# A graph-network kernel on one core: the opening layer norm in seven slices, the histogram finished inside the first pass, and two pieces of the second pass moved ahead of its scatter

## The chip, the cores and the metric

The kernel runs on one core of one Trainium2 chip. The metric is device microseconds (us) of one execution. Engines are named as in the profile: PE is the matrix engine, DVE the vector engine, ACT the scalar engine, POOL the GpSimd engine and SP the sync engine, which here only issues transfers. Every engine runs its own list of instructions in order and waits on semaphores for the others.

## What is computed

The graph has 12,500 nodes with 64 features and 212,500 directed edges, sorted by destination (`dst`). Edge attributes (32 numbers) and edge weights come with each edge. Four graph layers work on the layer-normed node features and are added up. What matters here:

```python
m = mean(x); h = relu((x - m) / sqrt(var(x) + 1e-5))        # opening layer norm, per node
# layer 0: max over the edges of a node, in both directions
edge = h[src] * (1 + coef * w)                               # and the same with src and dst exchanged
pooled = relu(edge @ pool_w.T + pool_b); pooled[src == dst] = -inf
agg = maximum(segment_max(pooled, other_end), 0)
x = x + relu(concat([h, agg]) @ final_w.T + final_b)
# layers 1 to 3 (not touched here): four dense graph convolutions, a message sum, an edge MLP
...
```

The kernel multiplies the node table by `pool_w` before the gather (the scale of an edge can be applied afterwards), and needs the edges once in order of `dst` and once in order of `src`; it sorts them itself by counting.

## The kernel before

The 12,500 nodes are padded to 98 blocks of 128 rows (`NJ = 98`), the edges to 1664 tiles of 128. An edge chunk is 8 tiles, so there are 208 chunks (`NCH = 208`, `NIT = 52` rounds of four). One indirect transfer of POOL moves one tile: 128 rows, with one row number per partition.

**Front.** SP queues all inputs, the whole `x` first (L499). DVE builds constants (L1961 to L1977), waits for every parameter, and then runs `norm(1)` (L1986) over all 98 blocks at once: sum, scale, subtract, square, sum, scale, reciprocal, multiply, with one square root on ACT. PE, ACT and DVE then project the normed rows by `poolw` in seven slices of 14 blocks (`project_pairs`, `pairs_in`, `pairs_out`), DVE copies each slice to `T` (L2041), and SP writes it to the table in HBM (L538). After that SP loads the first row numbers (L596), and DVE zeroes `Z` and splits the node numbers into digits of 7 bits (L2042 to L2054).

**Pass one** (`step1` on each engine, `gather_pass` on POOL and SP). For each chunk POOL gathers 8 tiles of the table (L833). DVE scales and masks them (`pre1`, L2085 and L2087), PE turns them (L969), ACT applies the relu (L1583), DVE takes a running maximum along runs of equal `dst` (`scan1`, L2070), PE turns them back (L978), ACT copies (L1510) and SP writes the rows (L557). In the same steps DVE builds one-hot rows of the digits for two half chunks (`onehots`, L2063), and PE adds them up as a histogram in two PSUM banks (`hist`, L1078). POOL may run up to four chunks ahead of `pre1` (`g_used`). ACT also queues, at every second chunk, zeros for the table `fill_rows` and for the adjacency matrix `adj` (`zeroes`, L1575 and L1570).

**Between the passes.** When the last chunk is done, PE closes the histogram (L1096), DVE turns counts into starts (L2115 to L2133, with PE at L1101 and L1106), and from these into row numbers (L2143 to L2155) and degrees (L2157 to L2162). POOL then scatters the 98 blocks of `T` to the first edge row of each node (`fill64`, L848). SP waits for that, copies one more row (L628), and starts the loads of pass two.

**Pass two** (`step2`). For each chunk SP loads rows of `fill_rows` (L637), masks (L551) and edge attributes (L646); DVE scans them (`scan2`), PE turns them (L1178), ACT scales them into records (`messages`, L1631) together with weights and digits (`payload`, L1612 to L1614). In parallel the *position chain* of a chunk finds where each record goes in the order by `src`: one-hot rows (L2173), PE products with the running counts (L1130 to L1156), ACT copies (L1620, L1626), DVE look-ups (L2190) and the integer row numbers (`pos`, L2200). POOL scatters the eight tiles of the chunk to `records` (L863). ACT's list has `payload` of a later chunk ahead of the second half of a chunk's messages, and `payload` waits for the scatter of the chunk that used the same of four buffers. After the first four chunks ACT writes the inverse degrees to HBM, 4 bytes at a time (L1668).

**After pass two** POOL gathers the ends of 98 blocks of runs of pass one into `T` (`ends`, L881), scatters 480 tiles of matrix cells to `adj` (L908), gathers the 98 blocks of run ends of pass three (L881), and scatters the other 1184 tiles. SP and DVE meanwhile read the records back, make the cells (`cells_made`, L2276 to L2331) and run pass three (`step3`). The dense layers read `adj`; their first group waits for the last cells (SP at L749, POOL's count at L900).

The order that matters most is POOL's own list:

```python
gather_pass("g_used", 0, 0, 16, TP)
pool.wait_ge(sem("fill_zero"), 16 * NCH // 2)
pool.wait_ge(*dve_at("rows_ready"))
# 98 indirect scatters to fill64, then 208 x scatter(it, i)
runs_done(1)
# wait for all records
ends(T, runs_l064, endrow[0], 0)
```

## Time and profile before

| | |
|---|---|
| three timed runs | 9992.73, 10000.24, 10000.26 us (median 10000.24) |
| the profiled execution, its own time | 9970.27 us |
| its span in the profile | 9968.5 us, so 1.8 us lie around it |
| first gather of pass one | 96.08 us |
| last gather of pass one, first fill scatter | 2226.94 us, 2254.86 us |
| last fill scatter, first record scatter | 2379.77 us, 2403.97 us |
| last record scatter, first run-end gather | 4539.48 us, 4542.60 us |
| last matrix cell | 6963.1 us |

A row of the timeline gives start, duration, engine, line, operation, tiles and count, and in brackets the idle time of the engine before it and what ended that. Times are counted from the start of the span.

### The profile page before, as it was taken

The numbers are of one execution on the slowest core, as the hardware profiler recorded it, in microseconds if no ns is written. First come the engines' busy times: TensorE is split into PE (matmuls) and PEld (weight loads), VectorE is DVE, ScalarE is ACT, GpSimd is POOL, SyncE is SP. The second block draws the span as 40 slices with busy tenths as digits, with TensorE's granted clock in tenths as the row PEclk, the third lists the DMA queues.
The fourth block names the chain that finished last, engine by engine and source line by source line (L and its number), as shares of the span: only waits on it lengthen the run. The fifth ranks groups of instructions, "written<-read, shape, count | busy, mean of one in ns | idle before, by whom it ended". The sixth has DMA issues, their size and how long they took to land.

```text
span 9968.5 us, 151706 instructions
## 1 busy us (share of the span) xinstructions
PE 7021.8 (70%) x44134; PEld 5746.9 (58%) x44134; DVE 7055.7 (71%) x18556; ACT 4861.0 (49%) x7947; POOL 5378.0 (54%) x5426
## 2 busy tenths in 40 slices
PE   3444444442888788782656567994899999997998
PEld 2333333332666667661445455662699898896787
DVE  6777777773766666663558777773788787787777
ACT  1111111111555555551542336883688787785777
POOL 4777777776777777777777777777000000000220
PEclk6555555556777766775876888997999999999999
DMA  4555555553333333339995896773788888886999
GB/s 147 167 170 173 167 170 167 169 165 49 93 92 94 93 92 93 92 94 80 274 235 122 196 214 176 203 204 86 200 281 280 249 281 256 273 282 179 209 216 198
DMA packets 2775231, 1739.56 MB, mean 175 GB/s; under 512 B 1805014, under 2 KB 2613948, under 8 KB 2774372
## 3 DMA queue, kind: packets, MB, share of 16 engines
q1 hardware_dynamic: 2435172, 1298.36, 51.7%
q10 hardware_dynamic: 165920, 277.72, 7.8%
q0 software_dynamic: 173408, 154.46, 6.6%
q8 instruction: 370, 6.06, 0.3%
q14 instruction: 361, 2.96, 0.1%
HBM read 1065.70 MB, written 506.69 MB: 158 GB/s over the span
## 4 chain that ended last, share of the span: by engine, by line
POOL 43%; PE 24%; issue 19%; DMA 7%; DVE 4%; ACT 2%; SPq 1%; POOLq 0%; DVEq 0%; ACTq 0%
PE PS L1307 16%; POOL adj L908 16%; POOL records L863 13%; POOL G L833 12%; PE PS L1497 3%; DMA pair_raw<-adj 2%; PE PS L1287 1%; DMA G<-node_table,IDX 1%; DMA raw_f<-adj 1%; ACT ring_f L1918 1%; DMA records<-RT,IDX 1%; POOL AG L881 1%; POOL T L881 1%; DMA IDX<-in_src_q 1%; DVE OH L2063 1%
## 5 line engine op out<-in xcount | busy, mean ns | idle before, releaser
L833 POOL DMA_INDIRECT G<-node_table,IDX x1664 | 1625.0, 977 | 601.5 <-issue 591.5
L908 POOL DMA_INDIRECT adj<-OH,EA x1664 | 1649.0, 991 | 507.4 <-issue 507.4
L863 POOL DMA_INDIRECT records<-RT,IDX x1664 | 1614.7, 970 | 545.0 <-issue 498.0
L1307 PE MATMUL PS<-ring_f,terms_r 128*128 128x448 f32 x8232 | 1701.1, 368 | 17.1 <-DVE ring_f L2569 10.8
L2569 DVE CAST ring_f<-raw_f 128x1792 fp32r<-128x1792 uint8 x1323 | 1404.9, 1091 | 376.0 <-DMA raw_f<-adj 186.3
L1795 ACT CAST ring_f<-raw_f 128x1792 fp32r<-128x1792 uint8 x882 | 1468.8, 1692 | 372.1 <-DMA raw_f<-adj 217.9
L1307 PEld LDWEIGHTS PS<-ring_f,terms_r 128*128 128x128 f32 x8232 | 1541.2, 188 | 166.1 <-DVE ring_f L2569 21.0
L1156 PE MATMUL PS<-R 98*128 98x128 f32 x3328 | 989.8, 390 | 0.0
L2070 DVE TENSOR_TENSOR_SCAN S<-M,S,PS 128x512 f32<-128x512 bf16 x621 | 790.9, 1274 | 229.3 <-ACT PS L1684 207.4
L1078 PE MATMUL PS<-OH 128*98 128x128 bf16 x3328 | 453.5, 317 | 630.2 <-DVE OH L2063 630.2
L927 POOL DMA_INDIRECT HC<-node_table,srow x21 | 30.5, 1450 | 1537.2 <-issue 1537.2
L2457 DVE SCALAR_TENSOR_TENSOR AG<-AG,PS 128x1792 bf16<-128x1792 uint8 x294 | 592.5, 2021 | 342.7 <-DMA AG<-adj 202.4
L2063 DVE TENSOR_SCALAR OH<-iota_b,AG 128x128 bf16<-128x128 bf16 (+1 forms) x4480 | 833.5, 284 | 0.0
L1078 PEld LDWEIGHTS PS<-OH 128*98 128x98 bf16 x3328 | 365.7, 198 | 796.7 <-DVE OH L2063 796.7
L2181 DVE TENSOR_TENSOR L<-PS,below 128x512 bf16<-128x512 f32 x416 | 285.4, 686 | 730.4 <-PE PS L1140 726.3
L1583 ACT ACTIVATE PS<-PS,poolb 128x512 f32<-128x512 f32 x208 | 137.7, 662 | 1252.7 <-PE PS L969 1189.4
L945 POOL DMA_INDIRECT ends_b<-runs_e,endrow_src x98 | 149.0, 1520 | 1049.8 <-PE PS L1319 547.9
L1156 PEld LDWEIGHTS PS<-R 98*128 98x128 f32 x3328 | 711.0, 264 | 0.0
L1154 PE MATMUL PS<-OH 128*98 128x128 bf16 x1664 | 473.0, 284 | 313.4 <-ACT R L1626 311.5
L1497 PE MATMUL PS<-ring_f,terms_r 128*128 128x448 f32 x2744 | 611.2, 377 | 68.8 <-DVE ring_f L2783 31.4
L1918 ACT CAST ring_f<-pair_raw 128x1792 fp32r<-128x1792 uint8 x343 | 571.6, 1693 | 170.1 <-PE PS L1497 109.8
L969 PE MATMUL PS<-ident,RT 128*128 128x128 f32 x832 | 231.8, 434 | 597.9 <-DVE RT L2087 596.9
(406 smaller groups left out, 14435.3 us busy)
## 6 DMA issues: line engine op xcount, KB each, us to landing
raw_f<-adj SPq DMA_DIRECT2D x2205, 224.0 KB, 3.6
adj<-Z ACTq DMA_DIRECT2D x105, 1568.0 KB
AG<-adj SPq DMA_DIRECT2D x735, 224.0 KB
G<-records SPq DMA_DIRECT2D x624, 128.0 KB
M<-same_dst SPq DMA_DIRECT2D x416, 128.0 KB
fill_rows<-Z ACTq DMA_DIRECT2D x104, 512.0 KB, 2.9
runs_l<-R SPq DMA_DIRECT2D x208, 256.0 KB
G<-fill_rows SPq DMA_DIRECT2D x208, 256.0 KB
```

Of the source, the lines that this page charges most:

```text
L833: pool.indirect_dma_start(G[:, i, q * D:(q + 1) * D], None, table, bass.IndirectOffsetOnAxis(ap=IDX[:, i, q:q + 1], axis=0)).then_inc(sem( ...
L863: pool.indirect_dma_start(rec, bass.IndirectOffsetOnAxis(ap=IDX[:, i, q:q + 1], axis=0), RT[:, i, q, :], None).then_inc(sem(f"scattered{i} ...
L908: pool.indirect_dma_start(adj_cells, bass.IndirectOffsetOnAxis(ap=CELL[:, at:at + 1], axis=0), VAL[:, at:at + 1], None).then_inc(sem(f"cel ...
L1078: t = pe.matmul(hist_of(b, k % 2 if b == 0 else 0), OH[:, s, 2 * b, k, 0:NJ], OH[:, s, 2 * b + 1, k, :], start=False, stop=False, skip_gro ...
L1156: t = pe.matmul(bank(6 + x)[:, k * P:(k + 1) * P], OHTs[0:NJ, x, k * P:(k + 1) * P], Cs[0:NJ, k, :], start=False, stop=True, skip_group_ch ...
L1307: m = pe.matmul(half_of(x, h)[:, c, :], stat, RINGF[q % NR][:, h * QW + c * HW:h * QW + (c + 1) * HW], start=K == 0, stop=False, skip_grou ...
L1497: m = pe.matmul(half_of(0, h)[:, c, :], stat, RINGF[n % NE][:, h * QW + c * HW:h * QW + (c + 1) * HW], start=p == 0, stop=p == AB - 1, ski ...
L1795: act.copy(RINGF[q % NR][:, :], RAWF[q % NW][:, :]).then_inc(sem("conv_a"), 1)
L1918: act.copy(RINGF[n % NE][:, :], raw[:, 0:2 * QW, K % 2]).then_inc(sem("conv_a"), 1)
L2063: t = dve.tensor_scalar(OH[:, s, d, k, 0:w], iota_b[:, 0:w], key(d, q + k), None, ALU.is_equal)
L2070: return dve.tensor_tensor_scan(S[:, i % 2, :], mask, data, init, op0, op1)
L2569: dve.tensor_copy(RINGF[q % NR][:, :], RAWF[q % NW][:, :]).then_inc(sem("conv_d"), 1)
```

## The change

1. **Front.** `x` is loaded in four parts, the first ahead of everything, with `poolw` after the second. The opening norm runs in seven slices of 14 blocks: DVE `centred` and `spread`, the square on ACT instead of DVE (`squared`), the root per slice, DVE `normed`; PE turns and projects a slice as soon as it is normed, and ACT instead of DVE copies the product to `T` (`pair_copied`). The first four loads of row numbers go ahead of the table writes. `DX`, the input of the same-run masks, lies in `Z` instead of `G`.
2. **Histogram.** Chunk `c` of pass one takes half chunks `HLO[c]` to `HLO[c+1]`, 9 for every 4 chunks, so all are done at chunk `CH = 185`; the counts become starts, row numbers and degrees in steps of chunks 185 to 192 (one call for each chunk). ACT's zeros of `fill_rows` go out in the first 104 chunks, those of `adj` at every second chunk as before.
3. **Extra row.** SP's copy of one row to `fill_rows` (with its two waits) moves from behind the fill scatter into round 39 of pass one; POOL's fill scatter waits for it.
4. **Position chains.** The chains of chunks 0 to 3, with their payloads and one-hot rows, come first in the lists of PE, DVE and ACT; the scans and messages of these chunks follow.
5. **Run ends.** POOL gathers the first 14 of the 98 run-end blocks between the fill scatter and the records, after a wait for the fill's landing; 84 stay behind the records.
6. Two helpers for ordering (`Steps`) are replaced by the common one (`then`), with the same waits.

```diff
-            load(X[:, :], a["x"])
+            x_in(0)
+            x_in(1)
+            sp.wait_ge(*dve_at("w_zero"))
+            for h in range(2):
+                sp.dma_start(poolw[h * D:(h + 1) * D, h * D:(h + 1) * D], a["poolw_t"]).then_inc(sem("x_in1"), 16)
+            x_in(2)
...
+            for i in range(4):
+                chunk_idx(i, i)
+            table_parts(UA)
             sp.wait_ge(*dve_at("md_ready"))
...
+                    if it == NIT * 3 // 4:
+                        sp.dma_start(dh[0:1, 0:1], a["dst_ext"][:, H + 1:H + 2]).then_inc(sem("dh_then_v"), 16)
...
+                        sp.dma_start(fill64[1:2, :], table[bass.ds(node_h, 1), :]).then_inc(sem("fill_b"), 16)
...
             pool.wait_ge(sem("fill_zero"), 16 * NCH // 2)
+            pool.wait_ge(sem("fill_b"), 16)
             pool.wait_ge(*dve_at("rows_ready"))
...
+            runs_done(1)
+            pool.wait_ge(sem("filled"), 16 * NJ)
+            ends(T, runs_l064, endrow[0], 0, 0, 2)
...
-            ends(T, runs_l064, endrow[0], 0)
+            ends(T, runs_l064, endrow[0], 0, 2, NG)
...
+            for s in range(NG2 + 3):
+                if s < NG2:
+                    squared(s)
+                if 1 <= s <= NG2:
+                    first_root(s - 1)
+                if 2 <= s <= NG2 + 1:
+                    pair_in(s - 2)
+                if s >= 3:
+                    pair_copied(s - 3)
...
+            for s in range(NG2 + 2):
+                if s < NG2:
+                    centred(s)
+                if 1 <= s <= NG2:
+                    spread(s - 1)
+                if s >= 2:
+                    normed(s - 2)
...
+            def step1(c):
+                pre1(c // 4, c % 4)
+                for h in range(HLO[c], min(HLO[c] + 1, HLO[c + 1])):
+                    onehots(h * KC, h % 2, h, 4)
+                if c:
+                    scan1((c - 1) // 4, (c - 1) % 4, c == 1)
+                for h in range(HLO[c] + 1, HLO[c + 1]):
+                    onehots(h * KC, h % 2, h, 4)
+                if c == CH + 1:
+                    starts_by_row()
...
+                payload(0, i, True)
+                for x in range(2):
+                    half(i, i, x, None, None, False)
+            for i in range(4):
+                act.wait_ge(sem("back2"), i + 1)
+                for q0 in range(0, 8 if i < 3 else 4, 2):
+                    messages(i, i, q0)
+            payload(1, 0, False)
             act.wait_ge(sem("oh_ready"), 2 * NCH + 1)
             act.dma_start(dinv_n.rearrange("o (j p) -> (o p) j", p=P), dinv[:, :], allow_slow_non_contiguous=True).then_inc(sem("dinv_out"), 16)
```

## Rows read from the trace of the kernel before

**Rows 1.** The page: POOL in 40 slices, and the chain that ended last.
```profile
POOL 4777777776777777777777777777000000000220
...
POOL 43%; PE 24%; issue 19%; DMA 7%; DVE 4%; ACT 2%; SPq 1%; POOLq 0%; DVEq 0%; ACTq 0%
```
**Rows 2.** The waits of POOL: us in total, times, longest us.
```profile
POOL fill_rows L848 <- DVEq L2156: 27.0, 1, 27.0
POOL records L863 <- ACT RT L1614: 23.2, 1, 23.2
POOL records L863 <- ACT RT L1631: 23.1, 27, 10.9
```
**Rows 3.** The lines of POOL's gathers and scatters: duration min/median/max, first and last start.
```profile
L833 POOL DMA_INDIRECT G<-node_table,IDX x1664: 940/944/2557, 96.1 to 2226.9; - x185
...
L863 POOL DMA_INDIRECT records<-RT,IDX x1664: 965/969/1048, 2404.0 to 4539.5; - x185
```
**Rows 4.** The timeline of the front, 0 to 135 us.
```profile
32.75 0.15 DVE L1981 TENSOR_SCALAR w12r<-w12c 64x1 f32<-64x1 f32 x1 [28.09 <-DMA wls<-in_ws]
...
35.15 6.68 DVE L1988 TENSOR_REDUCE nd<-X 128x98 f32<-128x6272 f32 x1
...
35.97 1.28 ACT L1554 ACT_TABLE_LOAD   x1
...
70.55 3.22 PE L1044 MATMUL PS<-ident,Hn 128*128 128x128 f32 x14 [35.21 <-DVEq L1998]
...
89.61 1.09 DVE L2041 TENSOR_SCALAR T<-PS 128x896 f32<-128x896 f32 x1 [0.47 <-PE PS L1037]
```
**Rows 5.** Busy time by stretch, 5 to 10 us: PE, PEld, DVE, ACT, POOL, clock, DMA, GB/s.
```profile
5.00:10.00 5.00, 0.00 (x0) 0.00 (x0) 0.00 (x0) 0.00 (x0) 0.00 (x0) 1.00 0.95 408
```
**Rows 6.** The timeline of DVE late in the kernel, a norm of one 14-block slice.
```profile
9105.35 1.09 DVE L2668 TENSOR_REDUCE nd<-X 128x14 f32<-128x896 f32 x1
9106.47 0.17 DVE L2669 TENSOR_SCALAR nd<-nd 128x14 f32<-128x14 f32 x1
...
9110.51 0.24 DVE L2675 RECIPROCAL nd<-na 128x14 f32<-128x14 f32 x1 [0.28 <-ACT na L1872]
```
**Rows 7.** Groups of ACT's instructions by shape: busy us, mean ns of one, idle before.
```profile
L1744 ACT ACTIVATE R<-Hn,pcols 128x896 f32<-128x896 f32 x20 | 22.7, 1134 | 29.8 <-DVEq L2432 28.4 <-DVEq L2532 1.4
...
L1533 ACT ACTIVATE G<-PS,pcols 128x896 f32<-128x896 f32 x7 | 7.7, 1097 | 17.1 <-PE PS L1044 17.1
```
**Rows 8.** The timeline of DVE near the end of pass one: two chunk starts.
```profile
2222.59 0.69 DVE L2085 TENSOR_TENSOR RT<-G,EA 128x512 f32<-128x512 f32 x1 [4.64 <-DMA G<-node_table,IDX]
...
2230.44 0.69 DVE L2085 TENSOR_TENSOR RT<-G,EA 128x512 f32<-128x512 f32 x1 [0.16 <-DMA G<-node_table,IDX]
```
**Rows 9.** The page's group of the one-hot rows of pass one (416 half chunks).
```profile
L2063 DVE TENSOR_SCALAR OH<-iota_b,AG 128x128 bf16<-128x128 bf16 (+1 forms) x4480 | 833.5, 284 | 0.0
```
**Rows 10.** The timeline behind the fill scatter: its last instruction, SP's first load.
```profile
2379.77 0.98 POOL L848 DMA_INDIRECT fill_rows<-T,begrow  x1 [0.30 <-issue]
...
2384.05 0.37 SPq L637 DMA_DIRECT2D G<-fill_rows  x1
```
**Rows 11.** DMA issues of 2380 to 2480 us: KB, us to landing.
```profile
dinv_n<-dinv ACTq DMA_DIRECT2D x1, 49.0 KB, 40.2
```
**Rows 12.** The timeline around the run ends: POOL's first gather, DVE's cells, POOL's first cell.
```profile
4542.60 0.98 POOL L881 DMA_INDIRECT T<-runs_l,endrow_dst  x1 [2.16 <-DMA records<-RT,IDX]
...
4643.38 0.56 DVE L2322 CAST OH<-EA 128x768 uint8<-128x768 int32 x1
...
4672.37 1.00 POOL L908 DMA_INDIRECT adj<-OH,EA  x1 [0.30 <-issue]
```
**Rows 13.** The timeline later: DVE's last step before POOL's second run ends, and these.
```profile
5231.06 0.17 DVE L2362 CAST dcol<-vcol 128x7 int32<-128x7 f32 x1
...
5291.72 0.99 POOL L881 DMA_INDIRECT AG<-runs,endrow_src  x1 [0.30 <-issue]
```
**Rows 14.** The waits of SP, 6000 to 7000 us.
```profile
SPq L749 <- POOLq L900: 126.3, 3, 79.0
```

More of the change, by code:

```diff
@@ L1080, in hist @@
                 t.then_inc(sem("hist_done"), 1)
-            def step1(it, i, first):
-                c = it * 4 + i
-                fwd(i, Gs[:, i % 2, :], c, sem("gs_ready"), c + 1)
-                hist(c * 2, 0)
-                if not (first and i == 0):
-                    back((i - 1) % 4, c - 1, c - 1)
-                hist(c * 2 + 1, 1)
-            for i in range(4):
-                step1(0, i, True)
-            for it in range(1, NIT):
-                for i in range(4):
-                    step1(it, i, False)
@@ L1109, in count_of @@
+            for c in range(NCH):
+                step1(c)
+            back(3, NCH - 1, NCH - 1)
             def count_of(h):
@@ L1189, in _ @@
             pe.wait_ge(*dve_at("starts_in"))
-            fwd2(0, 0)
             turn(0, 0)
@@ L1193, in _ @@
             for i in range(4):
-                step2(0, i, False)
+                for x in range(2):
+                    chain(i, i, x, False)
+            fwd2(0, 0)
+            for i in range(4):
+                back2(i, i)
+                fwd2((i + 1) // 4, (i + 1) % 4)
             for it in range(1, NIT - 1):
@@ new lines, in starts_in_all @@
+            def starts_in_all():
+                dve.wait_ge(*pe_at("row_offs"))
+                then(dve.tensor_copy(hoff[0:NJ, :], bank(5)[0:NJ, P:P + 2]))
+                for i in range(2):
+                    then(dve.tensor_tensor(HC[0:NJ, 2 + i, :], HC[0:NJ, 2 + i, :], HC[0:NJ, i, :], ALU.subtract))
+                    dve.tensor_scalar(HC[0:NJ, 2 + i, :], HC[0:NJ, 2 + i, :], hoff[0:NJ, i:i + 1], None, ALU.add)\
+                       .then_inc(sem("starts_ready"), 1)
+                dve.wait_ge(sem("starts_ready"), 2)
+                dve.tensor_tensor(HC[0:NJ, 4, :], HC[0:NJ, 4, :], HC[0:NJ, 3, :], ALU.add).then_inc(sem("starts_ready"), 1)
@@ L2136, in row_of, with starts_by_node @@
+            def starts_by_node():
+                dve.wait_ge(*pe_at("starts_t"))
+                for i in range(2):
+                    dve.tensor_copy(cnt[i][:, :], starts_of(i))
+                    then(dve.tensor_copy(beg[i][:, :], starts_of(2 + i)))
+                dve.sem_inc(sem("dve_at"), 1)
             def row_of(dst, e, w):
@@ new lines, in degrees, with step1 @@
+            def degrees():
+                dve.wait_ge(sem("root_out"), NG2 + 1)
+                then(dve.reciprocal(dinv[:, :], na[:, :]))
+            def step1(c):
+                pre1(c // 4, c % 4)
+                for h in range(HLO[c], min(HLO[c] + 1, HLO[c + 1])):
+                    onehots(h * KC, h % 2, h, 4)
+                if c:
+                    scan1((c - 1) // 4, (c - 1) % 4, c == 1)
+                for h in range(HLO[c] + 1, HLO[c + 1]):
+                    onehots(h * KC, h % 2, h, 4)
+                if c == CH + 1:
+                    starts_by_row()
+                if c == CH + 2:
+                    starts_in_all()
+                if c == CH + 3:
+                    starts_by_node()
+                if c == CH + 4:
+                    rows_of_nodes(0)
+                if c == CH + 5:
+                    rows_of_nodes(1)
+                if c == CH + 6:
+                    first_rows()
+                if c == CH + 7:
+                    degrees()
@@ L2165, in onehots2 @@
+            for c in range(NCH):
+                step1(c)
+            scan1(NIT - 1, 3, False)
             def onehots2(h, s):
@@ L2211, in scan2, with step2 @@
                 dve.sem_inc(sem("pt_free"), 1)
-            def step2(it, i, first, last):
+            def step2(it, i, last):
                 c = it * 4 + i
@@ L2216, in step2 @@
                 end = last and i == 3
-                scan2(it, i, first and i == 0)
-                if not (first and i == 0):
+                scan2(it, i, False)
+                if c != 4:
                     look(h - 1, c - 1, (i - 1) % 4, 1)
```

302 lines of the change are left out of this document (155 added, 147 removed).

## The prediction

> **What bounds the kernel now.** I read the page's slices and its chain first, then POOL's waits, then the timelines around each of those waits. In the slices POOL stands at seven tenths from 96 us to about 6960, and the chain gives POOL 43% and "issue" 19% [rows 1]. Seven tenths is POOL at its limit: one indirect transfer takes 0.944 (gather) or 0.969 us (scatter), and 0.30 us of issue follow each of them [durations in rows 3, the issue in rows 10], so a tile costs 1.247 to 1.27 us, and POOL has 1664 + 98 + 1664 + 98 + 1664 + 98 of them in a line. So up to 6963 us the time is set by POOL's list, and only holes in that list can be closed. POOL's waits show them: 27.0 us ahead of the fill scatter, 23.2 us ahead of the records, 23.1 us over 27 waits among the records, with one of 10.9 [rows 2]; besides, everything ahead of the first gather at 96.1 us [rows 3].
>
> **Front.** Now DVE idles 28.09 us until all parameters are there, then runs five operations of 6.68 us over all 98 blocks, one after the other, and only then PE and ACT begin [rows 4]. The change cuts this into seven slices. `x` is no limit: the loads run at 408 GB/s [rows 5], so the first slice (448 KB) is there at about 3 us and all of `x` (3136 KB) at about 10, while DVE's constants take it to 4.7. A slice costs DVE what a later norm of the same shape shows: 1.12 us for each big operation from start to start, 0.20 for a small one, 0.27 for the reciprocal [rows 6]. Without the square, that is four big, two small and a reciprocal, 4 x 1.12 + 2 x 0.20 + 0.27 = 5.1 us, and 36 us for seven. ACT has per slice a square (1.13, by its nearest row with a source in SBUF), a root (0.2), the relu (1.10) and the copy (0.9 to 1.1) [rows 7], together 3.5 us, so DVE sets the pace; a few waits where ACT's ordered list meets DVE's add about 2 us. DVE ends at 4.7 + 36 + 2 = 42.5. The last slice still goes through PE (1.6 us for seven products at the slow rate of 3.22 per 14 [rows 4]), the relu, PE again (1.4) and the copy, with hops 5 to 6 us: 48. Today the last copy ends at 90.7 [rows 4] and POOL starts 5.4 us behind it; the row numbers are loaded earlier now, but the table write has to land as before, so I keep 5 and put the first gather at 52.5. **Gain 43.5 us**, bounds 38 (waits in every slice) and 47 (none, and PE at its fast rate).
>
> ACT has run no Square in this trace. The trace shows one table load of 1.28 us when ACT first takes a root, and none when relus and copies follow [rows 4]. If Square and Sqrt lay in different sets, each slice would pay two loads, 2.56 us more on ACT, which then sets the pace; worked through the slices this ends 4 us later. The Trainium skill, "ScalarE: Activation LUTs", section "Table sets: the hidden batching unit", asks to group calls by set, which the slices would break; by its price of about 2.7 us a switch the front would end some 22 us later, an estimate. I take no load; the case is rival F.
>
> **Pass one.** The histogram's half chunks rise from 2 to 9/4 per chunk until chunk 185. DVE needs 7.85 us for a chunk when it doesn't wait (from 2222.59 to 2230.44 [rows 8]), and a half chunk of one-hot rows is 833.5 / 416 = 2.0 us of DVE [rows 9], 2.6 with its gaps. On average that makes 7.85 + 0.25 x 2.6 = 8.5 us, in a chunk with three halves 10.5, against POOL's 2131.8 / 208 = 10.25. POOL may be four chunks ahead, so one long chunk in four is covered, and the pass keeps POOL's pace. The number of one-hot rows is the same in all, so what they do to POOL (a mean of 977 ns against a median of 944) stays. The starts, row numbers and degrees move beside the gathers: some 45 small DVE instructions, about 13 us, which fill half of the 27.0 us gap now [rows 2]. They ran while POOL waited, so their effect on a gather is not in the trace; the nearest is the second half of the run ends, where 98 gathers take 129.8 us for 98 x 1.247 = 122.2 while DVE makes cells for 40 us [rows 12], 7.6 us lost. By that share I put 1.5 us on the starts and the position chains together; bounds 0 and, were POOL blocked for as long as DVE works, 13. SP's two waits for the extra row hold its list for some 5 us once; the row numbers are loaded three chunks (30 us) ahead, so nothing. Fill zeros in the first 104 chunks only move traffic, and DMA is not what POOL waits for; nothing.
>
> **Between the passes.** When the last gather ends, the row numbers are there since chunk 192, and the 27.0 us [rows 2] shrink to an issue gap: **gain 26.5 us**, unless DVE lags by 15 chunks.
>
> **Behind the fill scatter.** Its 98 tiles stay (126 us); the chains of four chunks lie beside them. At pass two's rate, 2135 us for 208 chunks [rows 3], four take 41 us, with pass one's last chunk ahead of them some 60, so they end long before. Today SP's first load goes 3.3 us after the last fill tile (the extra row is in it) and the first record 19.9 us after that load [rows 10, 3]. Now POOL waits some 1.5 us for the landing, then has 14 gathers of 1.247, 17.5 us, and could take records 19.3 us after the last fill tile. The messages must be ready by then: load, scan, turns and eight ACT operations. That took at most 1.8 + 19.9 = 21.7 us when the chain ran in between, and without the chain I estimate 12 to 13. So 19.3 against 23.2: **gain 3.9**, bounds 1.5 and 4.2. **The 14 gathers leave their old place: gain 17.5.** There POOL gets to the first cell scatter 17.5 us earlier against the records; today DVE has the cells ready at 4644 and POOL comes at 4672 [rows 12], so 28 us of cover less 17.5, still 10 in hand. At the second run ends DVE was done at 5231 and POOL came at 5292 [rows 13], 60 us in hand. At the end SP waits 126 us for cells [rows 14], so the dense layers take the whole shift.
>
> **The hole among the records.** The 10.9 us come at chunk 4, where ACT's `payload` waits for the scatter of chunk 1, which lands late because the inverse degrees, in pieces of 4 bytes, take 40.2 us to land [rows 11]. That transfer is still issued after four chunks, now as soon as chunk 0 has landed, some 4 us earlier against the records. I take a gain of 2, bounds 0 and 15.
>
> **Sum:** 43.5 + 26.5 + 3.9 + 17.5 + 2 - 1.5 = 91.9, so 92 us. Against the profiled execution's own 9970.27 that is 9878; the median of the runs is 30 us above it, and I set the gain against the median: 10000.24 - 92 = **9908 us**. What a measurement here can tell from no change is 0.2%, 20 us.
>
> **Rivals.**
> *A, a new wait takes the 17.5.* The cells come later than I think, because the read-back of the records now shares DMA with POOL's cell scatter. For it: only 10 us are in hand. Against it: the read of the first cells ends before POOL gets there. 10000.24 - 92 + 17.5 = 9926.
> *B, the hole closes.* If the late landing no longer meets ACT, all 15 us of it go: 10000.24 - 92 - 13 = 9895.
> *C, DVE blocks POOL.* If a transfer could not be issued while DVE works, 13 us of starts and four chains of about 7 us (some seven tenths of a chunk) would be paid in full, 41 us: 9948. Against it stands the record scatter: with a busy DVE its median is 969 ns and its longest of 1664 is 1048 [rows 3]; for it, a gather of 2557 ns [rows 3]. The Trainium skill, "SBUF — State Buffer", section "Who interferes with whom", speaks for it: a vector operation in a two-port mode, or with two inputs in SBUF, keeps GpSimd out for the whole instruction. By that rule it is the moved small operations, not the one-hot rows, that would cost.
> *D, the early histogram misses.* DVE lags so far that row numbers come at the old place: 26.5 back, 9935. DVE's 8.5 us against 10.25 speaks against it.
> *E, slower: DVE becomes pass one's bound.* If a chunk cost DVE over 10.25 us on average, POOL would wait for `g_used` in 185 chunks. It turns the change into a loss above 10.25 + 92 / 185 = 10.75; at 11 us the pass grows by 139 and the time is 10047. It needs 2.5 us a chunk that the timeline doesn't show.
> *F, ACT changes tables in every slice.* The 4 us above: 9912. Against it: relu and copy forced no load behind the root [rows 4]; Square itself is not shown.
>
> **How the numbers follow.** Forecast 0.64, F 0.06, A 0.10, B 0.09, C 0.05, D 0.04, E 0.02. The forecast's own terms spread from 38 to 47 in the front, from 0 to 13 in what DVE costs POOL; with A and B that makes 9885 to 9930. I widen it to 9880 to 9932, since the profiled execution lies 30 us under the median. All cases but E are faster by over 20 us: faster 0.96; E and some mixture of C, D and A leave 0.02 for no change and 0.02 for slower.
>
> **What would show it.** First gather near 52 us; the fill scatter right behind the last gather, with no wait; the first record about 19 us behind the last fill tile, with 14 gathers in between; 84 gathers behind the records and no wait ahead of the first cell; a mean of L833 that stays under 0.985 us. Wrong would be a POOL waiting for `g_used` in pass one (E), a mean of over 1 us (C), or a wait ahead of the cells (A).

## The result, and the profile after

The changed kernel takes 9901.15 us (median of 4 runs, 9889.59 to 9904.07), the kernel before 9998.43 us in the same rounds (4 runs, 9992.73 to 10000.26): a ratio of 0.9906, 95% interval 0.9894 to 0.9919, so 97 us less. The forecast was 9908, 92 us less than the 10000.24 known then. The profiled execution of the changed kernel took 9903.3 us, with a span of 9901.5.

Both kernels were profiled a second time later. From the starts of POOL's transfers every term of the forecast can be read as a difference; all times in us, the first and the second profile of each kernel side by side:

| term, start to start | before | changed | forecast | measured |
|---|---|---|---|---|
| first gather | 96.1, 96.2 | 55.0, 54.1 | 43.5 | 41.0, 42.1 |
| pass one, first to last gather | 2130.9, 2130.5 | 2139.4, 2134.5 | -1.5 | -8.5, -4.1 |
| last gather to first fill tile | 27.9, 28.0 | 1.2, 1.2 | 26.5 | 26.7, 26.7 |
| the 98 fill tiles | 124.9, 124.9 | 125.2, 125.2 | 0 | -0.3, -0.3 |
| last fill tile to first record | 24.2, 24.5 | 20.5, 20.5 | 3.9 | 3.7, 4.0 |
| first to last record | 2135.5, 2138.4 | 2133.4, 2130.9 | 2 | 2.1, 7.5 |
| last record to first adj cell | 132.9, 131.8 | 114.9, 114.6 | 17.5 | 18.0, 17.2 |
| first to last cell | 2290.7, 2290.2 | 2288.8, 2290.1 | 0 | 1.9, 0.1 |
| **up to the last cell** | 6963.1, 6964.4 | 6878.4, 6871.2 | **91.9** | **84.7, 93.2** |
| last cell to the end | 3005.4, 3020.0 | 3023.1, 3018.8 | 0 | -17.7, 1.2 |

The page of the changed kernel: the 40 slices of POOL, the chain that ended last, and the groups that answer to [rows 1, 3].

```profile
POOL 5777777777777777777777777776000000001220
...
POOL 43%; PE 19%; issue 18%; DMA 10%; DVE 5%; ACT 4%; SPq 1%; POOLq 0%; ACTq 0%; DVEq 0%
...
L853 POOL DMA_INDIRECT G<-node_table,IDX x1664 | 1633.5, 982 | 560.5 <-issue 548.7
...
L907 POOL DMA_INDIRECT records<-RT,IDX x1664 | 1614.9, 970 | 519.8 <-issue 497.7
```

POOL is still the bound up to the last cell: the same seven tenths and the same 43% of the chain. What is left of idle time shows in POOL's waits (us in all, times, the longest), which answer to [rows 2]:

```profile
POOL G L853 <- issue: 548.7, 1625, 53.7
...
POOL records L907 <- ACT RT L1677: 21.7, 30, 8.7
...
POOL T L884 <- DMA fill_rows<-T,begrow: 2.0, 1, 2.0
```

The wait of 27.0 us ahead of the fill scatter and that of 23.2 us ahead of the records are gone, the first gather waits 53.7 us instead of 95, and among the records there is still one of 8.7. The joints in POOL's timeline (start, duration; in brackets the idle time before it and its releaser):

```profile
2194.39 0.94 POOL L853 DMA_INDIRECT G<-node_table,IDX  x1 [0.30 <-issue]
2195.64 1.02 POOL L869 DMA_INDIRECT fill_rows<-T,begrow  x1 [0.30 <-issue]
...
2320.83 0.98 POOL L869 DMA_INDIRECT fill_rows<-T,begrow  x1 [0.30 <-issue]
2323.79 0.99 POOL L884 DMA_INDIRECT T<-runs_l,endrow_dst  x1 [1.98 <-DMA fill_rows<-T,begrow]
...
2340.10 0.94 POOL L884 DMA_INDIRECT T<-runs_l,endrow_dst  x1 [0.30 <-issue]
2341.35 1.00 POOL L907 DMA_INDIRECT records<-RT,IDX  x1 [0.30 <-issue]
...
4588.39 0.94 POOL L884 DMA_INDIRECT T<-runs_l,endrow_dst  x1 [0.30 <-issue]
4589.64 1.00 POOL L931 DMA_INDIRECT adj<-OH,EA  x1 [0.30 <-issue]
```

Every joint but the landing of the fill tiles is a bare issue of 0.30 us: the row numbers are there when the last gather ends, the messages when the 14 run ends are through, the cells when the other 84 are. So the parts of the change do what they say. Three rows of the table are off: the front gave 1.4 to 2.5 us less than forecast, pass one is 4 to 9 us longer, and in the first pair of profiles 18 us are missing behind the last cell, where the change does nothing. And one row, then as now, deserved more attention than it got: a mean gather of 0.982 us (0.977 before) against a median of 0.944 [rows 3] is 1664 x 0.038 = 63 us of pass one.

**Where those 63 us sit.** DVE and POOL around one long gather of the changed kernel, from the timelines of the two engines:

```profile
1004.54 0.69 DVE L2158 TENSOR_TENSOR RT<-G,EA 128x512 f32<-128x512 f32 x1 [4.29 <-DMA G<-node_table,IDX]
1005.26 0.69 DVE L2160 TENSOR_TENSOR RT<-RT,EA 128x512 f32<-128x512 f32 x1
1005.87 1.35 DVE L2136 TENSOR_SCALAR OH<-iota_b,AG 128x98 bf16<-128x98 bf16 x8
...
1004.25 0.94 POOL L853 DMA_INDIRECT G<-node_table,IDX  x1 [0.30 <-issue]
1005.49 1.28 POOL L853 DMA_INDIRECT G<-node_table,IDX  x1 [0.30 <-DMA IDX<-in_src_q]
1007.08 1.00 POOL L853 DMA_INDIRECT G<-node_table,IDX  x1 [0.30 <-issue]
```

The gather at 1004.25 was under way before the multiply began and took 0.94 us. The one at 1005.49 started inside the add, which had 0.46 us to run, and took 0.34 longer. Counted over all 1664 gathers: in 220 of them one of the two operations was running, or began, within 0.05 us of the gather's start, and these lose 57.1 us; the other 1444 lose 5.5. In the kernel before it is 46.8 us in 214, and 7.4 in the rest. The loss follows the time that the operation has left at the gather's start: 0.2 to 0.3 us left cost 0.12 on average, 0.4 to 0.5 cost 0.32, 0.6 to 0.7 cost 0.50; an operation that begins later in the gather costs 0.03 us at most. That this is a cause and not a coincidence, the first two experiments show.

### The profile page after: what moved, and what is told of

Read it like the earlier page. It is cut to its first block, busy times and chain, and to the rows that moved or that the text cites. A ratio compares the mean times of both kernels' runs of the same rounds, so it can differ in the third digit from the quotient of the medians.

```text
span 9901.5 us, 151767 instructions
## 1 busy us (share of the span) xinstructions
PE 7084.5 (72%) x44134; PEld 5794.4 (59%) x44134; DVE 7040.9 (71%) x18590; ACT 4876.1 (49%) x7967; POOL 5382.8 (54%) x5426
## 4 chain that ended last, share of the span: by engine, by line
POOL 43%; PE 19%; issue 18%; DMA 10%; DVE 5%; ACT 4%; SPq 1%; POOLq 0%; ACTq 0%; DVEq 0%
POOL adj L931 16%; POOL records L907 12%; PE PS L1342 12%; POOL G L853 12%; DMA raw_f<-adj 3%; DMA pair_raw<-adj 3%; PE PS L1532 2%; ACT ring_f L1848 2%; DMA G<-node_table,IDX 1%; DVE OH L2136 1%; PE PS L1322 1%; POOL fill_rows L869 1%; POOL T L884 1%; POOL AG L884 1%; DMA records<-RT,IDX 1%
## 5 line engine op out<-in xcount | busy, mean ns | idle before, releaser
L1342 PEld LDWEIGHTS PS<-ring_f,terms_r 128*128 128x128 f32 x8232 | 1534.4, 188 | 180.2 <-ACT ring_f L1848 24.5
L1187 PE MATMUL PS<-R 98*128 98x128 f32 x3328 | 1010.0, 397 | 0.0
```

The lines of the kernel that those rows point to most:

```text
L1187: t = pe.matmul(bank(6 + x)[:, k * P:(k + 1) * P], OHTs[0:NJ, x, k * P:(k + 1) * P], Cs[0:NJ, k, :], start=False, stop=True, skip_group_ch ...
L1342: m = pe.matmul(half_of(x, h)[:, c, :], stat, RINGF[q % NR][:, h * QW + c * HW:h * QW + (c + 1) * HW], start=K == 0, stop=False, skip_grou ...
```

## Experiments

Each kernel is the changed one with the edit named, unless it says otherwise. Spans and stretches are those of the kernel's own profile; beside them stand the times of the changed kernel's two profiles.

**1. Multiply and add of pass one on ACT.**

```diff
-                pre1(c // 4, c % 4)
...
+                scaled(c)
                 relu1(c % 4, c)
...
+                for q in range(8):
+                    t = act.activation(Gs[:, i % 2, q * D:(q + 1) * D], G[:, i, q * D:(q + 1) * D], ACT.Identity,
+                                       scale=s_q[:, c * 8 + q:c * 8 + q + 1], bias=pen_q[:, c * 8 + q:c * 8 + q + 1])
```

> The two DVE operations per chunk that multiply and add with both sources in SBUF (128x512 each, 0.69 us) become eight operations of 64 columns on ACT. Theory 1 (a DVE operation with two sources in SBUF holds up a gather that wants SBUF at its start or some 0.7 us into it; in the changed kernel 126 of 129 gathers of over 1.1 us overlap the add): the long gathers go, the mean of the 1664 gathers falls from 0.982 to about 0.95 us, pass one from 2139 to about 2090, the time to about 9852. Theory 2 (long gathers come from the DMA queues, the add only happens to follow a landing): mean and pass one stay within 5 us, the time at 9901. Where ACT became late, POOL would wait for the scaled chunks and the pass would be longer than 2139.

**2. The same on DVE with one source in SBUF.**

```diff
-                dve.tensor_tensor(o, g, bc(s_q[:, bass.ds(q, 8)], [P, 8, D]), ALU.mult)
-                dve.tensor_tensor(o, o, bc(pen_q[:, bass.ds(q, 8)], [P, 8, D]), ALU.add)
+                for k in range(8):
+                    t = dve.tensor_scalar(Gs[:, i % 2, k * D:(k + 1) * D], G[:, i, k * D:(k + 1) * D],
+                                          s_q[:, q + k:q + k + 1], pen_q[:, q + k:q + k + 1], ALU.mult, ALU.add)
```

> The multiply and the add of pass one become eight DVE operations of 64 columns with one source in SBUF and two scalars per partition. Theory 1 (only operations with two sources in SBUF hold a gather up): as with the work on ACT, a mean gather of about 0.95 us, pass one about 2090, the time about 9852. Theory 1b (any DVE operation does while it runs): the long gathers go, since each operation is some 0.1 us, but many gathers are longer by up to 0.1, a mean of about 0.96, pass one about 2105. Theory 2 (the DMA queues): no change, 2139 and 9901.

The group of the gathers on the page, with the work on ACT, then with one source on DVE:

```profile
L853 POOL DMA_INDIRECT G<-node_table,IDX x1664 | 1577.6, 948 | 561.1 <-issue 546.7
```

```profile
L853 POOL DMA_INDIRECT G<-node_table,IDX x1664 | 1579.6, 949 | 564.1 <-issue 540.8
```

The mean falls from 982 to 948 and 949 ns, and the gathers of over 1.1 us from 129 to 3 and 4. Pass one takes 2083.5 and 2092.3 us (of the latter some 5.5 us are waits of POOL for a chunk's row numbers), the time 9841.35 and 9847.5. So theory 1 holds: the two operations with both sources in SBUF cost pass one some 50 us. For the kernel before, where no run takes them away, the count above says 46.8. Theory 1b asked for a mean of 0.96 us and is out at that size: over the usual 0.944, all gathers together lose 8.8 us here and 6.8 with the work on ACT. That leaves some 2 us for the 1664 short operations, so a few nanoseconds for a gather are not excluded. The expectation named a second moment, 0.7 us into a gather; for these two operations the count above shows only the start, and what looked like the second was the multiply just ahead of the add. Longer operations with one source do have a second moment (experiment 7).

**3. The late histogram, twice.** Two half chunks per chunk, starts and row numbers behind pass one:

```diff
-        HLO = [min(2 * NCH, c * 9 // 4) for c in range(NCH + 1)]
-        CH = HLO.index(2 * NCH)
+        HLO = [2 * c for c in range(NCH + 1)]
+        CH = NCH - 1
...
             scan1(NIT - 1, 3, False)
+            starts_by_row()
...
+            degrees()
```

> The changed kernel with two half chunks of the histogram per chunk again and the starts, row numbers and degrees behind the last chunk of pass one; the front, the fill zeros, the chains and the 14 run ends stay as changed. Both theories: the gap between the last gather and the first fill tile comes back, from 1.2 to about 27 us. They differ on pass one, which took 2139.4 us in the changed kernel against 2130.9 before. Theory 1 (the extra DVE work of the early histogram moves DVE's operations against POOL's gathers, and more of them collide): the pass goes back to about 2131, the time rises by about 18 us to 9919. Theory 2 (the fill zeros, all in the first 104 chunks now, slow the gathers): it stays at about 2139, and the time rises by 27 us to 9928.

> The kernel with the late histogram once more. Its first pass one took 2137.3, but in that execution the median record scatter was 0.972 instead of 0.969, so all POOL work 0.3% longer, which is 5 us of that. Theory 1 (the early histogram shifts DVE's two-source operations against the gathers): with a record median of 0.969 pass one takes 2130 to 2133, as in the kernel before (2130.9 and 2130.5). Theory 2 (the fill zeros in the first half, or another part that stays changed here): 2135 to 2139, as in five profiles with the early histogram.

The gap comes back in full, in POOL's waits of the first run:

```profile
POOL fill_rows L868 <- DVEq L2222: 28.2, 1, 28.2
```

28.2 us where before has 27.0 [rows 2], so the histogram's term is confirmed. The times were 9940.43 and 9931.06, above what either theory said (9919 and 9928). Pass one took 2137.3 and 2132.4; all POOL work was some 0.3% longer in both executions (the median record 972 ns against 969 and 970), so the median of 0.969 that the second expectation asked for did not come. Leaving that out, the gathers that take over 0.02 us more than the usual 0.944 lose 57 and 52 us here, 56 to 62 in five profiles with the early histogram, and 54 and 53 in the two of the kernel before. That points to theory 1, at some 5 us, but the spread within one kernel is as large. What differs is a class of gathers that meet a whole operation (0.56 to 0.61 us longer, the multiply beginning at most 0.05 us behind their start): 26 and 25 in the two profiles of the changed kernel, none before, 10 and 4 here. Why the three-half chunks put the multiply there is not settled. Theory 2 has nothing for it: in the changed kernel's first profile the chunks 8 to 103, beside which the fill zeros run, lose 26.8 us, the chunks 104 to 199 lose 29.7.

**4. Both kernels once more**, with no edit.

> The kernel before, unchanged, profiled once more. In its first profiled execution the stretch behind the last adj cell took 3004 us and the whole 9970, 30 us under the median of its runs; the changed kernel's stretch took 3022, though the change does nothing there. Theory 1 (that first execution was a short one): behind the last cell now 3015 to 3030, up to the last cell 6964 within 5 us. Theory 2 (the change costs the dense layers 18 us): 3004 again, and the 30 us missing up to the last cell. The sum of the terms up to the last cell is the same by both, 84.7 us.

> The changed kernel, unchanged, profiled once more, for the spread of three terms. First gather: 55.0 in the first profile, 51.8 in two kernels with the same front, 55.6 in a third; if the last table write meets ACT's first adj zeros by chance, either value may come. Pass one: 2139.4; theory 1 (collisions of DVE's two-source operations with gathers come by phase) lets it fall anywhere from 2131 to 2141, theory 2 (the early histogram or the fill zeros cost 8 us) gives 2139 within 1.5. Behind the last cell: 3015 to 3030.

Behind the last cell, start of that cell to the end, the kernel before took 3020.0 us this time, the changed one 3018.8. So the 18 us missing there in the first pair are the short execution of the kernel before, and no cost of the change. Up to the last cell the two profiles of before agree within 1.3 us. The first gather of the changed kernel came at 54.1, pass one took 2134.5.

**5. No run ends ahead of the records.**

```diff
-            runs_done(1)
-            pool.wait_ge(sem("filled"), 16 * NJ)
-            ends(T, runs_l064, endrow[0], 0, 0, 2)
...
-            ends(T, runs_l064, endrow[0], 0, 2, NG)
+            runs_done(1)
+            ends(T, runs_l064, endrow[0], 0, 0, NG)
```

> The changed kernel with none of the 14 run-end gathers ahead of the records: all 98 come behind them again. Theory 1: POOL idles behind the last fill tile until the messages of chunk 0 are written, some 11.5 us (they were there at 2333.3, the last fill tile ended at 2321.8), so the first record comes 7.8 us earlier against the fill than with 14 gathers between, and the first cell 17.5 us later against the last record; together 9.7 us slower, about 9911. Rival (the two gains of the forecast are separate, 3.9 and 17.5): 21.4 slower, about 9922. What the 14 gathers are worth is the idle time that they fill, not their own length.

9910.99 us. POOL's waits behind the fill:

```profile
POOL records L904 <- ACT RT L1675: 20.5, 3, 11.6
```

POOL idles 11.6 us until the first messages are there, and the last record to the first cell takes 133.2 us again. From the last fill tile to the first record 12.6 us against 20.5, from the last record to the first cell 133.2 against 114.6: 18.6 - 7.9 = 10.7 us lost, near the 9.7 of theory 1. The 17.5 us that the forecast booked as one gain and the 3.9 that it booked as another are one thing: the 14 gathers fill 11.6 us of idle time, of which 2.0 go for the landing that they wait for.

**6. The inverse degrees written out beside the fill scatter.**

```diff
+            act.wait_ge(sem("oh_ready"), 2 * NCH + 1)
+            act.dma_start(dinv_n.rearrange("o (j p) -> (o p) j", p=P), dinv[:, :], allow_slow_non_contiguous=True).then_inc(sem("dinv_out"), 16)
             oht_copy(0, 0)
             for i in range(4):
                 payload(0, i, True)
...
             payload(1, 0, False)
-            act.wait_ge(sem("oh_ready"), 2 * NCH + 1)
-            act.dma_start(dinv_n.rearrange("o (j p) -> (o p) j", p=P), dinv[:, :], allow_slow_non_contiguous=True).then_inc(sem("dinv_out"), 16)
```

> The changed kernel with the write of the inverse degrees (pieces of 4 bytes, 40 us to land) issued beside the fill scatter instead of behind the messages of chunk 3. Theory 1 (the two holes among the records, 4.5 and 8.7 us, come because that write delays the landing of the records that ACT's payload waits for): both go, first to last record takes 2120 instead of 2133.4, the fill scatter stays at 125.2, and the time falls by 13 us. Rival (the write delays the fill tiles in the same way): the wait behind the last fill tile, 1.98 us, or the fill itself grows by as much. Rival 2 (the holes come from four chunks of messages being late by themselves): they stay.

POOL's waits from the fill to the last record:

```profile
POOL records L907 <- ACT RT L1677: 10.4, 34, 0.3
...
POOL T L884 <- DMA fill_rows<-T,begrow: 2.0, 1, 2.0
```

No wait among the records is longer than an issue any more, first to last record takes 2121.5 instead of 2133.4 and 2130.9, and neither the wait for the fill tiles nor the fill (125.5 against 125.2) has grown. So the holes were the landing of the 4-byte pieces [rows 11], as the forecast read them, and they cost 9 to 12 us. The time, 9898.41, shows less of it: the stretch behind the last cell, where the edit does nothing, took 3028.1 us against 3023.1 and 3018.8, and the cells before it 2292.0 against 2288.8 and 2290.1.

**7. The last layer's weights behind the table writes.**

```diff
-            load(l3w1[:, :], a["l3w1"])
-            load(l3w2[:, :], a["l3w2"])
...
             table_parts(UA)
+            load(l3w1[:, :], a["l3w1"])
+            load(l3w2[:, :], a["l3w2"])
```

> The two loads of the last layer's weights, whose issue takes SP 8 us, go behind the seven table writes in SP's list; DVE's digits and ACT's first adj zeros, which wait for the parameters, come some 10 us later with them. Theory 1 (the first gather comes at 55.0 instead of the 52.5 forecast because the table writes start at 33.5 where the first slice is ready at 26, and the last one shares DMA with the adj zeros): the writes start at about 26, the last lands 4 us after its issue at 45, the first gather at about 50, the time 4 to 5 us lower, 9897. Rival (a table write takes 10 us to land whatever is beside it): first gather at 55. What could go wrong: the digits end at about 71 instead of 59, and POOL, which can be four chunks ahead, would wait for the first scaled chunk if that came after about 91.

9894.93 us. The writes start at 28.3, the first gather comes at 51.7, but the first gathers are long. POOL, then DVE:

```profile
55.65 1.90 POOL L853 DMA_INDIRECT G<-node_table,IDX  x1 [0.30 <-issue]
57.85 3.30 POOL L853 DMA_INDIRECT G<-node_table,IDX  x1 [0.30 <-issue]
61.45 1.82 POOL L853 DMA_INDIRECT G<-node_table,IDX  x1 [0.31 <-issue]
...
57.54 1.55 DVE L2115 MEMSET Z<- 128x1792 f32 x1 [0.44 <-DVE vpos L2081]
59.01 0.96 DVE L2119 TENSOR_SCALAR AG<-EA 128x1664 int32<-128x1664 int32 x1
60.00 1.03 DVE L2121 CAST AG<-AG 128x1664 f32<-128x1664 int32 x1
61.06 1.03 DVE L2119 TENSOR_SCALAR AG<-EA 128x1664 int32<-128x1664 int32 x1
62.12 1.03 DVE L2121 CAST AG<-AG 128x1664 f32<-128x1664 int32 x1
```

The fill of `Z` and the digits, with one source or none, now run beside the first gathers and hold them up too: the first 64 lose 10.9 us in all, against 4.3 and 5.3 in the changed kernel. That is more than the 2.4 to 3.3 us that the front gave. (The gather at 55.65 met an operation with two sources, ahead of the fill, L2067.)

These operations hold a gather at two places. The one at 61.45 began when the operation at 61.06 had 0.64 us left. In the changed kernel a gather that began with as much left, and with no operation behind that one, took 1.45 us. This one took 1.82 and ended 0.12 us behind the cast that followed at 62.12. Among the first 40 gathers of the kernels with the front in slices there are 18 that began under a cast or scalar operation of about 1 us with another right behind it, and all 18 ended 0.12 us behind the second. Where an operation with two sources followed, the gather was no longer than the first operation alone would make it (1.51 us with 0.70 left).

**8. Three edits together (1, 6, 7), then a fourth: the square of the norm beside the cells on ACT.**

```diff
-                then(dve.tensor_tensor(AG[:, :], Hn[:, :], Hn[:, :], ALU.mult))
+            act.activation(AG[:, :], Hn[:, :], ACT.Square).then_inc(sem("squared"), 1)
             root(NG2 + 2)
```

> The changed kernel with the three edits together: multiply and add of pass one on ACT, the last layer's weights loaded behind the table writes, the inverse degrees written out beside the fill scatter. If they add up: first gather at about 51.7, pass one about 2084, no wait among the records (first to last 2121), so against the run with the work on ACT alone, 9841, another 3.9 for the front and 9.4 for the holes: 9828. If one of them takes from another (the digits come 12 us later with the loads, and ACT then has the first chunks to scale late), POOL waits in its first chunks and the time stays above 9835.

> The three edits, and in the norm beside the cell scatter the square of all 98 blocks (one DVE operation of 6.69 us with both sources in SBUF) goes to ACT. If such an operation holds POOL for its whole length here too, the stretch of 1056 adj cells, now 1374 to 1377 us with single transfers of up to 7.1 us, loses about 6 us and one of the three longest transfers, and the time is 6 us below the kernel with three edits, 9822, a step that the stretch shows and the times hardly do. If POOL's long transfers there have another cause, the stretch stays.

Three edits: 9836.97 us, ratio to before 0.9852 (0.9837 to 0.9867). Four: 9831.07, ratio 0.9849 (0.9836 to 0.9863). Both are clearly under the changed kernel's 0.9906; one from the other can't be told by the times. No wait of over 0.3 us is left among gathers and records. The fourth edit is read in the timelines. First DVE and POOL in the changed kernel:

```profile
5420.40 6.69 DVE L2071 TENSOR_REDUCE nd<-X 128x98 f32<-128x6272 f32 x1
5427.37 6.69 DVE L2073 TENSOR_TENSOR Hn<-X,nd 128x6272 f32<-128x6272 f32 x1
5434.10 6.69 DVE L2074 TENSOR_TENSOR AG<-Hn 128x6272 f32<-128x6272 f32 x1
5440.82 6.69 DVE L2075 TENSOR_REDUCE nb<-AG 128x98 f32<-128x6272 f32 x1
5449.15 6.69 DVE L2079 SCALAR_TENSOR_TENSOR Hn<-Hn,nd 128x6272 f32<-128x6272 f32 x1
...
5428.50 6.40 POOL L931 DMA_INDIRECT adj<-OH,EA  x1 [0.30 <-issue]
5435.21 6.42 POOL L931 DMA_INDIRECT adj<-OH,EA  x1 [0.30 <-issue]
5441.93 0.96 POOL L931 DMA_INDIRECT adj<-OH,EA  x1 [0.30 <-issue]
5449.57 7.12 POOL L931 DMA_INDIRECT adj<-OH,EA  x1 [0.31 <-issue]
```

Three operations with two sources, three transfers that end 0.8 us behind them; the two reductions, just as long with one source, hold nothing (the transfer at 5441.93 lies inside one and takes 0.96). With the square on ACT two long transfers are left:

```profile
5360.01 6.71 POOL L931 DMA_INDIRECT adj<-OH,EA  x1 [0.30 <-issue]
...
5379.74 7.30 POOL L931 DMA_INDIRECT adj<-OH,EA  x1 [0.30 <-issue]
```

The transfer that met the square is gone: the three long ones were 17.0 us over the median of 0.969 in all, the two are 12.1, which makes 5 of the 6 us expected. The stretch of the 1056 cells between the second run ends and the last 128 cells says it less clearly: it takes 1372.1 us, and 1369.1 in the next kernel, which has the edit too, but 1372.6 to 1377.4 in the nine profiles without it in which POOL runs at its usual pace (1375.8 and 1375.3 in the changed kernel).

The page of the changed kernel holds the same hint for all cells, a mean above the median of 969 ns:

```profile
L931 POOL DMA_INDIRECT adj<-OH,EA x1664 | 1651.3, 992 | 507.3 <-issue 507.3
```

38 cells take over 1.2 us, together 38.0 us more than the median, and every one of them begins under, or within 0.05 us of, a DVE operation with two sources. The fourth edit removes one of these operations; the others were not tried.

**9. ACT's first zeros of adj later**, with edits 1, 6 and the square, the loads in their old order:

```diff
-            for k in range(2 * NIT, AB):
-                adj_zero(k * P)
...
             def zeroes(c):
+                if c == 0:
+                    for k in range(2 * NIT, AB):
+                        adj_zero(k * P)
```

> The kernel with the square on ACT too, but with the order of the loads as in the changed kernel and ACT's first zeros of adj (1568 KB, issued at 45 to 47 beside the last table write) issued behind the first chunk's relu instead. Theory 1 (in the changed kernel the first gather comes at 55 where these zeros reach the DMA queues together with the last table write, at 51.8 where they come behind it): first gather at 50 to 52. DVE's digits, which with the loads moved ran beside the first gathers and made them up to 3.3 us long, lie ahead of them again, so that the first 64 gathers lose 4 to 6 us to long transfers instead of 11, and the time is some 5 us under 9831: 9826, less than the times can tell. Rival (the table write itself varies): first gather at 54 to 56.

9838.46 us, ratio 0.9851 (0.9834 to 0.9867), the same as the two before within their spread. The first gather came at 52.1, with the last copy at 46.8, and the first 64 gathers lose 4.2 us, both near what was expected. What separates the 12 profiles of the front in slices is the time from the end of the last copy to the first gather. In the four kernels without the zeros beside the table writes it is 5.2 to 5.4 us every time (as in 44.94 to 50.33 below, ACT's last copy and POOL's first gather with three edits); in the eight with them it is 5.2 to 5.3 three times and 7.6 to 10.5 five times (10.1 in the changed kernel's first profile, 44.95 to 55.04, the second fence). Only this experiment moves the zeros alone, and it is one profile, so the zeros are the likely cause and not a shown one.

```profile
44.03 0.91 ACT L1581 COPY T<-PS 128x896 f32<-128x896 f32 x1 [0.66 <-PE PS L1060]
...
50.33 1.10 POOL L853 DMA_INDIRECT G<-node_table,IDX  x1 [48.99 <-issue]
```

```profile
44.04 0.91 ACT L1581 COPY T<-PS 128x896 f32<-128x896 f32 x1 [0.66 <-PE PS L1060]
45.08 0.67 ACTq L1623 DMA_DIRECT2D adj<-Z  x1
...
33.52 12.62 SPq L553 DMA_DIRECT2D node_table<-T  x7
...
55.04 1.21 POOL L853 DMA_INDIRECT G<-node_table,IDX  x1 [53.70 <-issue]
```

## Why the prediction was right, and where it was not

The time, 9908 against 9901.15, came out of terms that mostly hold one by one. Some of its closeness is luck: the front and pass one fell 4 to 9.5 us short, the records gave up to 5.5 more than forecast, and the runs show 97 us where the two pairs of profiles show 84.7 and 93.2 up to the last cell.

**Front.** Forecast 52.5, measured 51.8 to 55.6 over the eight profiles in which the front is as changed. DVE set the pace as worked out, and the last copy ended at 45 to 46.6, earlier than the 48 forecast: DVE was through at 39.8 to 41.5 instead of 42.5 (4.8 us a slice where it did not wait, against 5.1), and the copy ended 5.1 us behind it instead of 5.5. (48 and 5 make 53; the 52.5 that was booked is half a microsecond less.) The step that failed is "the table write has to land as before, so I keep 5": it is 5.2 to 5.4 where the 1568 KB of zeros come later, but 7.6 to 10.5 in five of the eight profiles in which the faster front brings them to the same moment. The prediction did not count this meeting, and experiment 9 makes it the likely cause. *Rival F* fell. Both kernels load a table at 0.76; behind that there is one more load, between the first slice's square and root, and none in the other six slices:

```profile
9.59 0.95 ACT L1563 ACTIVATE AG<-Hn 128x896 f32<-128x896 f32 x1 [1.38 <-DVE Hn L2040]
10.56 1.28 ACT L1568 ACT_TABLE_LOAD   x1
11.85 0.21 ACT L1568 ACTIVATE na<-nb 128x14 f32<-128x14 f32 x1
```

The Trainium skill ("ScalarE: Activation LUTs", "Table sets: the hidden batching unit") puts about 2.7 us on a switch; this one took 1.31 us from the end of the square to the root, and square, root, relu and copy ran on without another.

**Between the passes**: 26.5 forecast, 26.7 measured, and 28.2 of wait back with the late histogram. *Rivals D and E* fell with it; POOL's waits for DVE in pass one are 0.3 us at most.

**Pass one.** The step that failed is "The number of one-hot rows is the same in all, so what they do to POOL (a mean of 977 ns against a median of 944) stays", with -1.5 for what moves; measured -4.1 and -8.5, inside the bounds 0 to 13. That mean was read as a price of the one-hot rows. It is the price of the multiply and the add, and it goes when these leave DVE (experiments 1 and 2). The operations that moved cost next to nothing: 49 gathers run beside the starts, row numbers and degrees (12.6 us of DVE) and lose 1.6 us, the 15 of them that meet one of these operations 0.1. The 1.5 was scaled from the run ends, where 98 gathers lost 7.6 us beside the cells that DVE makes, and there too it is mostly operations with two sources that hold the gathers up. The longest of them in the kernel before, POOL and then DVE:

```profile
4627.56 2.41 POOL L881 DMA_INDIRECT T<-runs_l,endrow_dst  x1 [0.30 <-issue]
...
4627.46 1.76 DVE L2303 TENSOR_TENSOR_SCAN EA<-ones 128x768 f32<-128x768 f32 x1
```

So the row that gave the price also held the mechanism. What makes pass one longer by 4 to 9 us is open (experiment 3).

**Rival C**, which the forecast gave 0.05, was rejected for the wrong reason. As priced there (41 us for the moved operations) it did not come: the fill scatter with four chunks' position chains beside it takes 125.2 us against 124.9, and the starts cost what was just said. But its mechanism is in the trace of both kernels, and worth more than that: 50 us of pass one. The row that was held against it, the longest record scatter of 1048 ns with a busy DVE, only shows that the DVE operations of that pass are of another kind (their second source is in PSUM, or they have one). The Trainium skill, "SBUF — State Buffer", "Who interferes with whom", makes this very distinction: a DVE operation with two SBUF sources keeps out a GpSimd instruction that reads SBUF, reductions never do, and casts and scalar operations can in a two-port mode. The trace agrees on each of these points: two sources cost up to 0.60 us a gather of pass one and made cell scatters 6.4 to 7.3 us long, 6.69 us of reduction cost nothing, and casts and scalar operations of about 1 us at the front made gathers up to 1.88 us long. The prediction counted by this rule only the operations that move, and not the multiply and the add, which have two SBUF sources in both kernels.

**Behind the fill scatter and the 14 run ends**: 3.9 and 17.5 forecast, 3.7 to 4.0 and 17.2 to 18.0 measured; *rival A* fell, no wait came ahead of the cells. But the reason given for the second was incomplete: moving work that the bounding engine does anyway gains only the idle time that it fills, here 11.6 us less 2.0 of landing (experiment 5). The sum of the two terms was right all the same, because the old stretch had 23.2 us of idle time [rows 2]: half of it went with the chains, which now run beside the fill, and with SP's first load, which comes 1.17 us behind the last fill tile instead of 3.30 (no run parts the two); the gathers took most of the rest.

**The hole among the records**: a gain of 2 forecast, 2.1 and 7.5 measured, with its cause as stated: the longest hole went from 10.9 to 8.7 us in the first pair of profiles and from 11.4 to 5.7 in the second. *Rival B*, that the change closes it, fell. Experiment 6 closes it with an edit of its own.

**The dense layers** took the whole shift, as forecast, once both kernels are profiled twice.

## What to carry to other kernels

Look at the mean against the median of the bounding engine's instructions, not only at its waits: 33 ns on each of 1664 gathers was a larger reserve than any hole in the list, and no wait in the profile named it; then look what the other engines run at the start of the long ones. Beside GpSimd's indirect transfers, give a DVE operation with two SBUF sources to ACT, or make it short ones with scalars per partition (64 columns here; operations of 1664 columns with one source held gathers up as well). And where a stage is made faster, list what else will be in the DMA queues at its new end; a bulk write that nobody waits for can go behind it, which cost nothing here (experiment 9).

## What the runs showed of the hardware that was not expected

- An indirect transfer is held up by a two-source DVE operation only if that operation runs at the transfer's start; one that begins 0.1 us later or more costs 0.03 us at most. The transfer then ends as much later as the operation had left, less about 0.13 us. Where both begin within 0.05 us of each other, either can be the one that waits: in the changed kernel's first profile 15 of the 416 operations take 0.71 to 0.77 us instead of the usual 0.69, and the gather at their start takes its usual 0.94.
- Long one-source operations at twice the pace per column (1664 columns in 1.03 us, where the two-source operations take 512 in 0.69) and a fill of 1792 columns held gathers up as well, the former at the gather's start and again near its end; a reduction of 6272 columns did not hold a cell scatter up.
- The same program's first gather came at 55.0 in one execution and 54.1 in another, and in kernels with the same front anywhere from 51.8 to 55.6: a single profile is not enough to read 3 us off this front.
